# A transformer layer on one core: the values of four head groups in one go, five buffers of transposed probabilities, rotation sums in place, and a new order of the pass on all engines

## The reference

```
n = layernorm(h)
q, k, v = n @ Wq (32 heads of 32), n @ Wk, n @ Wv (8 groups of 4 heads share a k and a v)
q, k = rotary(q), rotary(k)
attn = softmax(causal(q @ k.T / sqrt(32)))
h = h + (attn @ v) @ Wo
m = layernorm(h);  low = m @ A;  w = 8 * softmax(m @ Wr + br)
h = h + 2 * sum_h w_h * (low_h @ B_h)
```

## Time and profile before

| | before |
|---|---|
| median of three runs | 2467.23 us |
| profiled execution, its span | 2466.1 us, 2464.3 us |
| PE busy | 2328.5 us (94%) |
| PE weight loads busy | 1228.2 us (50%) |
| DVE busy | 1945.1 us (79%) |
| ACT busy | 1847.7 us (75%) |
| POOL busy | 1651.9 us (67%) |
| DMA queue q1, share of the 16 engines' time | 90.0% |
| chain that ended last | PE 69%, DVE 14% |
| granted TensorE clock, 360 to 2300 us | 1.00 (2.4 GHz) |

### The profile page before, as it was taken

The page is one execution under the profiler, slowest core; times in us unless marked ns, Lnnn a source line. Parts: engine busy times, 40 slices in busy tenths (PEclk is TensorE's granted clock), DMA queues, the critical chain, the costliest instruction groups (busy, mean ns, idle before and its releaser), DMA issues.

```text
span 2464.3 us, 58944 instructions
## 1 busy us (share of the span) xinstructions
PE 2328.5 (94%) x18704; PEld 1228.2 (50%) x18704; DVE 1945.1 (79%) x7924; ACT 1847.7 (75%) x6398; POOL 1651.9 (67%) x1529
## 2 busy tenths in 40 slices
PE   3998589999999999999999999999999999999986
PEld 2777244444555444455544445554544545454443
DVE  8999368887877788787778888777888887888864
ACT  5988277777777777777777777777777777777773
...
GB/s 71 265 255 243 100 146 168 187 183 187 186 183 176 184 185 184 187 187 184 175 181 187 185 185 187 184 176 181 186 184 186 187 183 177 181 186 184 185 164 99
DMA packets 1199526, 443.65 MB, mean 180 GB/s; under 512 B 1149552, under 2 KB 1151856, under 8 KB 1199216
## 3 DMA queue, kind: packets, MB, share of 16 engines
q1 hardware_dynamic: 1199216, 439.89, 90.0%
...
## 4 chain that ended last, share of the span: by engine, by line
PE 69%; DVE 14%; issue 2%; ACT 2%; POOL 1%; DMA 1%; SPq 0%; POOLq 0%; DVEq 0%; ACTq 0%
PE pb L852 8%; PE pb L854 7%; PE pb L853 7%; PE pa L852 6%; PE pa L853 6%; PE pa L854 6%; PE pc L852 4%; PE pv_ps L881 4%; PE pc L854 4%; PE pc L853 4%; PE s_ps L866 4%; DVE pr L1146 2%; DVE bn L1165 2%; DVE h L1256 2%; DVE nrm L1179 2%
## 5 line engine op out<-in xcount | busy, mean ns | idle before, releaser
L1003 ACT ACTIVATE pr<-pr,smin 128x128 f32<-128x128 f32 x2048 | 792.9, 389 | 113.8 <-DVE smin L1146 113.5
L1360 POOL TENSOR_TENSOR p<-pr,p 128x512 f16<-128x512 f32 x512 | 600.6, 1173 | 252.5 <-ACT p L1013 242.3
L1352 POOL TENSOR_TENSOR pr<-pr,rinv 128x512 f32<-128x512 f32 x512 | 529.4, 1039 | 270.3 <-DVE rinv L1154 270.3
L1013 ACT ACTIVATE p<-pr 128x512 f16<-128x512 f32 x512 | 319.6, 624 | 235.2 <-POOL pr L1352 218.7
L1146 DVE CUSTOM_DVE_ANT_0 pr<-s_ps,cst 128x128 f32<-128x128 f32 x2048 | 471.7, 285 | 26.1 <-POOL p L1360 14.1
L1003 ACT ACTIVATION_READ_ACCUMULATOR pr<-pr,smin 128x1 f32 x2048 | 383.8, 187 | 0.0
L611 PE MATMUL hps<-z,xw 128*128 128x256 f32 x848 | 194.0, 389 | 61.9 <-POOL xw L321 42.2
L866 PEld LDWEIGHTS s_ps<-kt,qt 128*128 128x128 f16 x2048 | 152.7, 98 | 144.4 <-DVE smin L1146 44.5
L852 PE MATMUL pa<-wkv_hi,xt 128*128 128x512 f16 x512 | 196.9, 385 | 26.8 <-DMA xt<-xs 26.8
L1200 DVE TENSOR_TENSOR xs<-h_ln,xs 128x512 f16<-128x512 f32 x128 | 123.5, 966 | 124.9 <-ACT xs L1048 124.9
L866 PE MATMUL s_ps<-kt,qt 128*128 128x128 f16 x2048 | 199.9, 221 | 16.1 <-DVE smin L1146 9.6
...
## 6 DMA issues: line engine op xcount, KB each, us to landing
h<-hout SPq DMA_DIRECT2D x128, 256.0 KB, 3.9
...
pt<-p SPq DMA_TRANSPOSE x512, 3.4
...
```

The source lines that it names most:

```text
L1003: last = A.activation(p, p, ACT.Exp, bias=smin[g % 2][:, j:j + 1], scale=-1.0, accum_out=rsum[g % 2][:, j:j + 1])
L1013: A.activation(p16[g % 2][:, 0:HG * P], pr[g % 2][:, :], ACT.Copy).then_inc(ph_done, 1)
L1352: nc.gpsimd.tensor_tensor(p3, p3, rinv[g % 2][:, :].unsqueeze(2).broadcast_to([P, HG, P]), ALU.mult).then_inc(p_norm, 1)
L1360: nc.gpsimd.tensor_tensor(p[:, HG * P:], pr[g % 2][:, :], p[:, 0:HG * P], ALU.subtract).then_inc(pl_done, 1)
```

## The change

The values of four groups come from one call (two calls per block instead of four), into all 512 columns of `pv_ps`; `ctx_high` and `ctx_low` copy 512 columns, twice per block. The transposed probabilities have five buffers, given out in turn over all groups of all blocks (`slot`), where there were four. The sums of the rotations are written over `rt_c` and `kt_c`, so `qr` and `kr` go, and with them the wait moves: `q_rotate` and `kv_rotate` on DVE now wait until ACT and POOL have split the sum before. `residual1` gets a wait on `h2_done` of two blocks earlier. The five lists are laid out anew. The lines of the new lists are all shown (a plus marks those that are new at their place); those they replace stand above. Also renamed in `q_high_a/b`, `k_high`, `q_low`, `k_low`: `qr` to `rt_c`, `kr` to `kt_c`.

```diff
-RP = 4
+RP = 5
...
-        qr = sb("qr", [P, 512])
...
-        kr = sb("kr", [P, G * HD])
...
+        def slot(b, g):
+            return (G * b + g) % RP
+
         def landed(eng, b, g):
-
-            reached(eng, pt_in[g % RP], 16 * (G // RP), b, 16 * (g // RP + 1))
+            n = G * b + g
+            if n >= 0:
+                eng.wait_ge(pt_in[n % RP], 16 * (n // RP + 1))
...
@@ sync: def p_transpose(b, g) @@
     reached(sp, pl_done, G, b, g + 1)
     pb_, pg = group(b, g - RP)
-    reached(sp, pv_done, G // 2, pb_, pg // 2 + 1)
-    sp.dma_start_transpose(pt[g % RP][:, :, :], p16[g % 2][:, :]).then_inc(pt_in[g % RP], 16)
+    reached(sp, pv_done, G // 4, pb_, pg // 4 + 1)
+    sp.dma_start_transpose(pt[slot(b, g)][:, :, :], p16[g % 2][:, :]).then_inc(pt_in[slot(b, g)], 16)
...
@@ sync: new order @@
 def body(i, odd):
+    x2_transpose(i - 2)
     p_transpose(i, 1)
+    p_transpose(i, 2)
+    x_transpose(i + 2, odd)
+    load_res(i - 1)
+    p_transpose(i, 3)
+    p_transpose(i, 4)
     k_transpose(i + 1, 0)
     q_transpose(i + 1, 0)
+    load_ln(i + 3)
     p_transpose(i, 5)
+    p_transpose(i, 6)
+    store(i - 3)
+    q_transpose(i + 1, 1)
+    p_transpose(i, 7)
+    p_transpose(i + 1, 0)
     k_transpose(i + 1, 1)
...
@@ tensor: def values(b, m, odd) @@
-    reached(pe, ctxl_done, G // 2, b, m)
-    for g in (2 * m, 2 * m + 1):
+    reached(pe, ctxl_done, G // 4, b, m)
+    for g in range(4 * m, 4 * m + 4):
         landed(pe, b, g)
-        to = slice(P * (g % 2), P * (g % 2) + P)
+        to = slice(P * (g % 4), P * (g % 4) + P)
...
@@ tensor: def wo_half @@
-        reached(pe, ctxl_done, G // 2, b, k // 2 + 1)
+        reached(pe, ctxl_done, G // 4, b, k // 4 + 1)
...
@@ tensor: new order @@
 def body(i, odd):
+    values(i - 1, 0, 1 - odd)
+    kv(i + 1, 1 - odd, 1, 2)
+    q_half(i + 1, 1 - odd, 0, 0, 1)
+    scores(i - 1, 7)
+    kv(i + 1, 1 - odd, 2, 3)
     q_half(i + 1, 1 - odd, 1, 0, 1)
+    kv(i + 1, 1 - odd, 3, 4)
+    ls_transpose(i - 3)
+    scores(i, 0)
+    q_half(i + 1, 1 - odd, 0, 1, 3)
+    scores(i, 1)
+    q_half(i + 1, 1 - odd, 0, 3, 7)
+    kv(i + 1, 1 - odd, 4, 5)
+    scores(i, 2)
+    q_half(i + 1, 1 - odd, 0, 7, 8)
+    out_half(i - 3, 0)
+    q_half(i + 1, 1 - odd, 1, 1, 2)
+    kv(i + 1, 1 - odd, 5, 8)
+    out_half(i - 3, 1)
     scores(i, 3)
+    q_half(i + 1, 1 - odd, 1, 2, 3)
+    wo_half(i - 1, 1 - odd, 1, 0, 2)
+    values(i - 1, 1, 1 - odd)
+    q_half(i + 1, 1 - odd, 1, 3, 4)
     wo_half(i - 1, 1 - odd, 0, 0, 1)
+    q_half(i + 1, 1 - odd, 1, 4, 5)
     scores(i, 4)
     q_half(i + 1, 1 - odd, 1, 5, 6)
+    wo_half(i - 1, 1 - odd, 0, 1, 4)
     scores(i, 5)
+    wo_half(i - 1, 1 - odd, 1, 2, 4)
+    wo_half(i - 1, 1 - odd, 0, 4, 8)
     scores(i, 6)
     low(i - 2)
+    wo_half(i - 1, 1 - odd, 1, 4, 6)
+    q_half(i + 1, 1 - odd, 1, 6, 8)
+    wo_half(i - 1, 1 - odd, 1, 6, 7)
+    kv(i + 2, odd, 0, 1)
+    wo_half(i - 1, 1 - odd, 1, 7, 8)
...
@@ scalar: def ctx_high(b, m, odd) @@
-    reached(act, pv_done, G // 2, b, m + 1)
+    reached(act, pv_done, G // 4, b, m + 1)
...
-    A.activation(ctx_t[odd][:, 2 * m:2 * m + 2, :], pv_ps[:, 0:2 * P].rearrange("p (g q) -> p g q", g=2),
+    A.activation(ctx_t[odd][:, 4 * m:4 * m + 4, :], pv_ps[:, :].rearrange("p (g q) -> p g q", g=4),
                  ACT.Copy).then_inc(ctxh_done, 1)
...
@@ scalar: new order @@
 def body(i, odd):
     exps(i, 1)
+    exps(i, 2)
     norm_root(0, i + 2)
     p_high(i, 1)
     norm_apply(0, i + 2, None)
     p_high(i, 2)
     x_high(0, i + 2)
+    ctx_high(i - 1, 1, 1 - odd)
+    exps(i, 3)
     exps(i, 4)
     v_high(i + 1, 1 - odd)
+    k_high(i + 1)
+    p_high(i, 3)
     q_high_a(i + 1)
     p_high(i, 4)
     exps(i, 5)
     exps(i, 6)
     p_high(i, 5)
+    router_exp(i - 2)
     p_high(i, 6)
+    q_high_b(i + 1)
     exps(i, 7)
+    norm_root(1, i - 1)
+    ls_high(i - 2)
+    exps(i + 1, 0)
+    ctx_high(i, 0, odd)
+    p_high(i, 7)
+    norm_apply(1, i - 1, 1 - odd)
+    p_high(i + 1, 0)
+    x_high(1, i - 1)
...
@@ vector: def ctx_low(b, m, odd) @@
-    V.tensor_tensor(ctx_t[odd][:, G + 2 * m:G + 2 * m + 2, :],
+    V.tensor_tensor(ctx_t[odd][:, G + 4 * m:G + 4 * m + 4, :],
...
@@ vector: def kv_rotate(b) @@
-    reached(dve, k_sum, 1, b)
+    reached(dve, kh_done, 1, b)
+    reached(dve, kl_done, 1, b)
...
@@ vector: def q_rotate(b, half) @@
-    reached(dve, q_sum, 2, b, half)
+    pb_, ph = (b, 0) if half else (b - 1, 1)
+    reached(dve, qh_done, 2, pb_, ph + 1)
+    reached(dve, ql_done, 2, pb_, ph + 1)
...
@@ vector: def residual1(b, half, odd) @@
+    reached(dve, h2_done, 2, b - 2, half + 1)
...
@@ vector: new order @@
 def body(i, odd):
+    mask_min(i, 0)
+    reciprocals(i - 1, 7)
+    q_double(i, 1)
+    norm_refine(1, i - 2)
+    reciprocals(i, 0)
     norm1_stats(i + 2)
+    ctx_low(i - 1, 0, 1 - odd)
+    ls_low(i - 3)
     mask_min(i, 1)
     x_low(1, i - 2, 0)
+    mask_min(i, 2)
     x_low(1, i - 2, 1)
     reciprocals(i, 1)
+    q_rotate(i + 1, 0)
+    reciprocals(i, 2)
     norm_refine(0, i + 2)
+    kv_rotate(i + 1)
+    residual2(i - 3, 0, 1 - odd)
     mask_min(i, 3)
+    x_low(0, i + 2, 0)
+    x_low(0, i + 2, 1)
+    residual2(i - 3, 1, 1 - odd)
+    mask_min(i, 4)
+    reciprocals(i, 3)
+    ctx_low(i - 1, 1, 1 - odd)
+    reciprocals(i, 4)
+    mask_min(i, 5)
+    mask_min(i, 6)
     k_double(i + 1)
+    reciprocals(i, 5)
+    q_double(i + 1, 0)
     router_max(i - 2)
     reciprocals(i, 6)
     residual1(i - 1, 0, 1 - odd)
     q_rotate(i + 1, 1)
+    residual1(i - 1, 1, 1 - odd)
     mask_min(i, 7)
     router_weights(i - 2)
...
@@ gpsimd: def sum_q(b, half) @@
-    reached(pool, qh_done, 2, pb_, ph + 1)
-    reached(pool, ql_done, 2, pb_, ph + 1)
-    nc.gpsimd.tensor_tensor(qr[:, :], rt_c[:, :], rt_s[:, :], ALU.add).then_inc(q_sum, 1)
+    nc.gpsimd.tensor_tensor(rt_c[:, :], rt_c[:, :], rt_s[:, :], ALU.add).then_inc(q_sum, 1)
...
@@ gpsimd: new order @@
 def body(i, odd):
+    q_low(i, 1)
+    v_low(i, odd)
     normalise(i - 1, 7)
+    normalise(i, 0)
     p_low(i - 1, 7)
     p_low(i, 0)
     normalise(i, 1)
+    normalise(i, 2)
+    p_low(i, 1)
     sum_k(i + 1)
+    p_low(i, 2)
+    sum_q(i + 1, 0)
+    normalise(i, 3)
+    normalise(i, 4)
+    p_low(i, 3)
     k_low(i + 1)
     p_low(i, 4)
     q_low(i + 1, 0)
     normalise(i, 5)
     normalise(i, 6)
     p_low(i, 5)
     sum_q(i + 1, 1)
     p_low(i, 6)
```

More of the change, by code:

```diff
@@ L881, in values @@
                                 last = pe.matmul(pv_ps[j * HD:(j + 1) * HD, to], v[:, g * HD:(g + 1) * HD],
-                                                 pt[g % RP][:, lo + j, :], start=(n == 0), stop=(n == 2))
+                                                 pt[slot(b, g)][:, lo + j, :], start=(n == 0), stop=(n == 2))
                     last.then_inc(pv_done, 1)
@@ L957, in body @@
-                    wo_half(i - 1, 1 - odd, 1, 1, 2)
-                    wo_half(i - 1, 1 - odd, 0, 1, 2)
-                    out_half(i - 3, 1)
                     q_half(i + 1, 1 - odd, 1, 5, 6)
-                    values(i - 1, 3, 1 - odd)
-                    wo_half(i - 1, 1 - odd, 1, 2, 3)
+                    wo_half(i - 1, 1 - odd, 0, 1, 4)
                     scores(i, 5)
-                    wo_half(i - 1, 1 - odd, 0, 2, 4)
-                    wo_half(i - 1, 1 - odd, 1, 3, 5)
+                    wo_half(i - 1, 1 - odd, 1, 2, 4)
@@ L966, in body @@
+                    wo_half(i - 1, 1 - odd, 0, 4, 8)
                     scores(i, 6)
-                    wo_half(i - 1, 1 - odd, 0, 4, 5)
-                    values(i, 0, odd)
                     low(i - 2)
-                    wo_half(i - 1, 1 - odd, 1, 5, 6)
-                    q_half(i + 1, 1 - odd, 1, 6, 7)
-                    wo_half(i - 1, 1 - odd, 0, 5, 8)
-                    values(i, 1, odd)
-                    q_half(i + 1, 1 - odd, 1, 7, 8)
-                    scores(i, 7)
@@ L976, in body @@
-                    kv(i + 2, odd, 0, 2)
-                    wo_half(i - 1, 1 - odd, 1, 6, 8)
-                    kv(i + 2, odd, 2, 5)
-                    scores(i + 1, 0)
-                    q_half(i + 2, odd, 0, 0, 2)
-                    kv(i + 2, odd, 5, 6)
-                    ls_transpose(i - 2)
-                    scores(i + 1, 1)
-                    kv(i + 2, odd, 6, 7)
-                    scores(i + 1, 2)
-                    q_half(i + 2, odd, 0, 2, 5)
-                    values(i, 2, odd)
@@ L1096, in body @@
                 def body(i, odd):
-                    norm_root(1, i - 2)
-                    ctx_high(i - 1, 1, 1 - odd)
-                    norm_apply(1, i - 2, odd)
-                    p_high(i - 1, 7)
-                    exps(i, 0)
-                    x_high(1, i - 2)
-                    ctx_high(i - 1, 2, 1 - odd)
-                    p_high(i, 0)
-                    ls_high(i - 3)
                     exps(i, 1)
+                    exps(i, 2)
                     norm_root(0, i + 2)
                     p_high(i, 1)
```

(17 more changed lines are left out.)

74 lines of the change are left out of this document (10 added, 64 removed).

## The result

The changed kernel takes 2477.07 us, the median of 7 runs (2473.26 to 2479.41), against 2466.64 for the kernel before in its 7 runs (2463.80 to 2468.26). The ratio is 1.004, with a 95% interval of 1.0029 to 1.0052: slower by 10 us, which is more than the 0.2% that a measurement tells from no change, and above the predicted range. The profiled execution took 2477.36 us, its span 2475.6.

A forecast was written before the change was run, and what follows sets the result against it. PE was taken as the bound: 33.20 - 0.38 - 0.43 + 0.25 + 0.10 = 32.74 us a pass, gaining 28.5 us over some 62 passes; with +2 at the edges, likeliest 2440 us, range 2411 to 2470.

The forecast's parts named there:

- Part 1, calls of `values`: On PE, two calls a pass in place of four save entry and exit twice, 2 x 0.19 = 0.38 us a pass.
- The two old stalls: PE's waits ahead of `wo_half` half 1 (0.20 us) and `scores(i+1, 2)` (0.23), together 0.43 us a pass, go.
- The stall at `ls_transpose`: New PE wait for DVE's `router_weights`, now behind `mask_min(i-1, 7)`: ready at 4.6 us against 4.35, 0.25 us a pass.
- `wo_half` half 1: PE needs `q_rotate(i+1, 0)`, ready near 14.9 us plus handoff and wanted at 15.3; 0.10 us a pass charged for slips.
- "All covered, by 0.5 to 1 us": `ctx_low(i-1, 1)`, both halves of `residual1` and their PE receivers: all in time; `ctx_low` ends near 22.9 us, wanted at 23.7.
- the rival of the residual load: SP's `load_res` behind `x_transpose` lands late, PE waits at `kv` and q half 0: 2480 to 2500 us; chance 10%.
- The rival "DVE blocked by POOL": `norm_refine` and `x_low` meet POOL, `q_rotate` comes 0.8 us late, PE waits 0.5: 2462 to 2470 us; chance 14%.
- Each wait as one chain from PE's clock: Method: PE's new list laid end to end, then each wait followed singly for whether its data are ready in time.
- The prediction's last sentence: Says the prediction is wrong if two engines' waits close into a loop that no single chain shows; no size.
- SP's queue and the buffers: With five buffers, SP's transpositions wait for `values`; this costs nothing, with some 3 us of cover at `p_high(i, 7)`.
- Sums in place, "nothing": DVE's rotations waiting for the earlier split instead of the sum cost nothing, since the splits end well before.
- Fill and drain: The first and last passes, where PE is not the bound: bounded by -4 and +8 us, taken as +2.

The follow-up runs named there:

- experiment 8: Kernel of experiment 5 with each four-group call of `values` cut into two calls of two, one k-step between them: 2447.09 us, ratio 0.9929 to the kernel before.
- experiment 5: Changed kernel with POOL's `sum_q(i+1, 0)` moved ahead of `sum_k(i+1)` and `p_low(i, 2)`, nothing left out: 2411.89 us, ratio 0.9777 to the kernel before.
- Experiments 1: Changed kernel with `ctx_low(i-1, 1)` moved up on DVE to right behind the two `x_low` of the first norm: 2512.10 us, ratio 1.0185 to the kernel before.
- 7: Changed kernel with `ctx_low(i-1, 1)` moved up, `router_weights` ahead of `mask_min(i, 7)` and `sum_q(i+1, 0)` moved earlier on POOL: 2434.32 us, ratio 0.9868.
- experiments 4: Changed kernel with six buffers of transposed probabilities in place of five: 2477.41 us, ratio 1.0042 to the kernel before.
- 9: Kernel before, order untouched, with five buffers alone: 2466.23 us; with the rotation sums in place alone: 2469.23 us; with both: 2473.28 us.

## Why the prediction was wrong

By its own steps:

- **Part 1, calls of `values`: right.** Two calls a pass at 0.88 us each against 0.89 laid out. Entry and exit cost 0.20 in experiment 8 against 0.19. In experiment 5, where PE has no stall left, a pass is 32.35 us; 33.20 less the 0.38 of the calls and the 0.43 of the old stalls is 32.39.
- **The two old stalls: right.** Neither `smin` nor `rt_s` at half 1 of the projection holds PE any more, and the 0.10 us of slip at `wo_half` half 1 did not come.
- **The stall at `ls_transpose`: right in place and size,** 0.25 us each. Its terms as written (2.2 + 0.39 + 0.85 + 1.08) give 4.52 and not 4.6, so 0.17 us; the 0.08 between are the two handoffs, from PE to DVE and back, which the trace has (0.03 and 0.05). And the 1.08 us from the earlier trace rows hold 0.59 for `w<-e`, a duration that changed with the order: 0.24 in experiment 5, where the stall is gone.
- **`wo_half` half 1: right, with luck.** DVE was there in time, since two errors cancel: `norm_refine` of the second norm took 1.48 us in place of 1.15, and the two `x_low` behind it 1.21 in place of 1.6.
- **"All covered, by 0.5 to 1 us": the step that failed.** It has `x_low(0)` end near 20.5 us into the pass (in the rival of the residual load); in the trace it ends at 22.3. It puts the end of `ctx_low(i-1, 1)` 22.9 us into the pass. In the trace it is at 1223.23 + 0.66 - 1199.46 = 24.4, and PE stood still for 0.67 us. Where the prediction shows its walk along DVE's list, two `x_low` are 1.6 us and a `norm_refine` 1.15; those of the first norm take 2.41 and 2.26 in the new order. Together that is 1.9 us more, on an engine whose cover was said to be 0.5 to 1; `ctx_low` is late by 1.5, since a few other terms came out shorter than laid out. The durations came from the earlier trace rows, where another order had set what POOL does beside them, and the term was carried over as if it belonged to the instruction. The Q sum moved away from `x_low` gives the whole loss back, with the 1.1 us at `norm_refine` left as they are (experiment 5).
- **The rival "DVE blocked by POOL": right in mechanism, wrong in place and size.** It looks for the price at `q_rotate` and `wo_half` half 1, at 0.5 us. There the meeting that it names came, and PE didn't wait: the first instruction of `norm_refine` takes 1.00 us beside `normalise`. The pause of POOL that it names as an argument against itself was there too, for the two `x_low` of that stretch (0.69 us each, POOL idle for 2.18). The price came at the other norm, for which the rival has no line: `sum_q` stands exactly beside its `x_low`. I had the order of POOL's list before me, and did not lay it against DVE's in time. It gives a pass of 33.1 to 33.2 us; it was 33.4.
- **Each wait as one chain from PE's clock: wrong in kind.** The prediction lays out PE's list, then asks of each receiver if it is in time. That holds as long as PE is the bound. Once DVE's list between two waits for PE is longer than the time that PE leaves, the pass is as long as the ring, and everything that PE saves becomes idle time. So the gain of 0.38 and 0.43 us did not go into smaller terms; it was all there on PE, and was spent waiting. Experiments 1 and 7 show the ring: 0.6 us put ahead in DVE's list lengthen the pass by 0.61, or by 0.37 where there is slack. The prediction's last sentence names such a loop as what would make it wrong, but does not look for one.
- **SP's queue and the buffers: right** (experiments 4 and 9). SP does wait for `values`, 15.6 us over twelve passes; PE never waits for `pt`, and ACT's `p_high` 2.0 us in all. The rival of the late residual load did not happen, although `x_low(0)` was later than the 1 us that it names: in the traced pass the load is issued at 1223.8 and lands at most 5.1 us later, and `residual1`, late itself, starts at 1230.72.
- **Sums in place, "nothing": wrong by 3.6 us.** In the traced execution most of it comes in two passes in which DVE and POOL meet for longer (experiment 9).
- **Fill and drain: +2 was on the wrong side.** The pass accounts for 62 x 0.21 = 13 us of loss, the median moved by 10.4: the edges gave back some 2.6 us, inside the bounds of -4 and +8. The upper time of the sum, 2462, is worked out with +2 and not with the +8 that the prediction bounds; with it, it is 2468, still below the 2477.

In the sum, a pass of 32.74 lacks 0.67 us for `ctx_low` and 0.10 for the two small stalls, and has 0.10 too much at `wo_half`: 33.41.
